# Second and third batch's extensions run back to back in two PSUM banks, and the third's sums are moved into the second's unit

## What is computed

```python
y = einsum('bti,oi->bto', x, W) + b + 2 * einsum('btr,bro->bto', einsum('bti,bir->btr', x, A[slot]), B[slot])
logits = einsum('bsd,ed->bse', y, route_w)
topk_v, topk_idx = top_k(logits, 1)
route_weight = one_hot(topk_idx[..., 0], 8) * topk_v
h = einsum('bsd,erd->bser', y, A2)
out = x + einsum('bser,eor->bso', route_weight[..., None] * h, Bw)
```

## Time and profile before

| | |
|---|---|
| Median of three executions | 285.2 us |
| The profiled execution | 284.73 us |
| Its span in the trace | 282.9 us |
| Mean granted TensorE clock | 0.998 of full speed |
| TensorE matmul, weight load | 277.5 us, 220.6 us busy |
| VectorE, ScalarE, GpSimd | 200.5, 110.2, 15.0 us busy |
| HBM read, written | 54.60 MB, 33.55 MB |

### The profile page before, as it was taken

How to read it: one execution, slowest core, us unless ns; L and a number is a source line. 1 busy time by engine, 2 the same in 40 slices (tenths; PEclk the granted TensorE clock), 3 DMA queues, 4 the chain that set the end, 5 groups by cost and what they waited for, 6 DMA issues and landing times.

```text
span 282.9 us, 4102 instructions
## 1 busy us (share of the span) xinstructions
PE 277.5 (98%) x1602; PEld 220.6 (78%) x1602; DVE 200.5 (71%) x223; ACT 110.2 (39%) x151; POOL 15.0 (5%) x46
## 2 busy tenths in 40 slices
PE   8999999999999999999999999999999999999993
PEld 5999999997676885788588758867885888588882
DVE  0052100077498999699879969996998799788794
ACT  0001201197685542744275346426533743370000
POOL 7600030000000000000000000000000000000000
PEclk9999999999999999999999999999999999999999
DMA  7999999999991076949966993999399759606598
GB/s 241 400 408 396 398 411 412 378 397 414 422 423 82 14 285 204 389 142 385 400 263 226 426 389 152 351 402 398 139 368 396 322 173 423 284 14 259 226 379 323
DMA packets 19014, 88.50 MB, mean 313 GB/s; under 512 B 2346, under 2 KB 4530, under 8 KB 11442
## 3 DMA queue, kind: packets, MB, share of 16 engines
q1 hardware_dynamic: 15696, 83.70, 75.3%
q10 hardware_dynamic: 3298, 4.54, 4.4%
HBM read 54.60 MB, written 33.55 MB: 312 GB/s over the span
## 4 chain that ended last, share of the span: by engine, by line
PE 93%; DVE 5%; ACT 0%; issue 0%; DVEq 0%
PE bank_out L641 16%; PE bank_eh L753 11%; PE bank_eh L769 10%; PE bank_eh L786 10%; PE bank_eh L741 10%; PE bank_out L721 9%; PE bank_out L714 9%; PE bank_out L705 9%; DVE x_ring L625 4%; PE bank_rl L641 3%; PE bank_eh L641 3%; PE bank_rl L679 1%; PE bank_eh L668 1%; PE bank_eh L792 1%; PE bank_rl L791 1%; PE bank_rl L797 1%
## 5 line engine op out<-in xcount | busy, mean ns | idle before, releaser
L393 ACT ACTIVATE x_hi<-x_ring 128x1024 fp32r<-128x1024 f32 x64 | 67.3, 1061 | 54.2 <-PE bank_eh L786 53.8
L489 DVE TENSOR_TENSOR x_lo<-x_ring,x_hi 128x1024 fp32r<-128x1024 f32 x64 | 77.6, 1221 | 8.5 <-ACT x_hi L393 8.5
L578 DVE TENSOR_TENSOR x_ring<-bank_out,x_ring 128x1024 f32<-128x1024 f32 x54 | 65.8, 1218 | 2.9 <-PE bank_out L721 2.7
L753 PE MATMUL bank_eh<-x_hi,m_hi 128*128 128x512 f32 x128 | 50.7, 396 | 0.0
L769 PE MATMUL bank_eh<-x_lo,m_hi 128*128 128x512 f32 x128 | 49.9, 390 | 0.0
L786 PE MATMUL bank_eh<-x_hi,m_lo 128*128 128x512 f32 x128 | 49.8, 389 | 0.0
L705 PE MATMUL bank_out<-wh_hi,bw_hi 128*128 128x512 f32 x120 | 46.7, 389 | 0.0
L714 PE MATMUL bank_out<-wh_lo,bw_hi 128*128 128x512 f32 x120 | 46.7, 389 | 0.0
L721 PE MATMUL bank_out<-wh_hi,bw_lo 128*128 128x512 f32 x120 | 46.7, 389 | 0.0
L641 PE MATMUL bank_out<-pt,w_ring 128*128 128x136 f32 x288 | 34.6, 279 | 0.0
L641 PEld LDWEIGHTS bank_out<-pt,w_ring 128*128 128x128 f32 x288 | 33.9, 190 | 0.1
(11 more groups left out here) (91 smaller groups left out, 211.4 us busy)
## 6 DMA issues: line engine op xcount, KB each, us to landing
x_ring<-xT SPq DMA_DIRECT2D x32, 1024.0 KB, 7.1
outT<-x_ring SPq DMA_DIRECT2D x26, 1024.0 KB, 4.9
w_ring<-W SPq DMA_DIRECT2D x28, 512.0 KB, 11.0
outT<-x_ring SPq DMA_DIRECT2D x5, 512.0 KB, 2.8
outT<-x_ring ACTq DMA_DIRECT2D x4, 512.0 KB, 2.9
w_ring<-W SPq DMA_DIRECT2D x6, 256.0 KB, 5.7
outT<-x_ring SPq DMA_DIRECT2D x5, 256.0 KB, 2.6
x_ring<-loraB ACTq DMA_DIRECT2D x8, 128.0 KB, 10.4
```

The costliest lines, as they stand in the source:

```text
L393: act.activation(out, in_, ACT.Copy).then_inc(done, 1)
L489: dve.tensor_tensor(out, a, b, ALU.subtract).then_inc(done, 1)
L578: dve.tensor_tensor(x, out_bank(b, j)[:, :, :], x, ALU.add).then_inc(v_out, 1)
L753: mm(bank_h, m_hi[:, c, :], hi, start=(c == 0), stop=False)
```

## The change

The batches are counted from 0, so the second and third are b = 1 and b = 2 (`TWIN`). The extension of b = 2 is moved from its own unit to directly behind that of b = 1. For that the extensions use two banks by turns: even batches the old `bank_e`, odd ones what was `bank_r`. The counts go to `bank_l`, over the logits. Top, sum_two, odd, sum_all, the copies to `e_st` and split_e of b = 2 leave the unit of b = 2 and are done in the unit of b = 1, top and sum_two at j = 3 (`TWIN_AT`), odd and sum_all at j = 4, the copies and split_e at j = 5. On ScalarE each of these stands ahead of the part's other work, on VectorE behind it. On VectorE the split of pair 3 of batch 2 is put behind weigh of batch 1. Waits on TensorE follow: the one for weigh of batch 1, which stood in the extension of b = 2, is now ahead of the last matmul of output pair 7 of batch 0; those of the counts' bank are merged with those of the logits.

```diff
@@ -162,8 +162,7 @@
...
         bank_rl = psum("bank_rl", [P, 2, T])
-        bank_e, bank_h = bank_eh[:, 0, :], bank_eh[:, 1, :]
-        bank_r, bank_l = bank_rl[:, 0, :], bank_rl[:, 1, :]
+        bank_e, bank_h, bank_l = (bank_eh[:, 0, :], bank_rl[:, 0, :]), bank_eh[:, 1, :], bank_rl[:, 1, :]
         bank_out = [psum(f"bank_out{i}", [P, 2, T]) for i in range(2)]
@@ -226,6 +225,7 @@
...
         EHI_AT, ELO_AT = 1, 1
+        TWIN, TWIN_AT = 2, 3
         LOG_AT, COPY_AT, AHEAD_AT, COUNT_AT, W_AT = 3, 4, 5, 6, 7
@@ -422,8 +422,8 @@
...
                     act.wait_ge(t_pb, 1)
-                    copy(pb[:, E:XN], bank_r[0:1, 0:PN], a_bp)
-                    copy(pb[:, 0:E], bank_r[0:1, 0:E], a_bp)
+                    copy(pb[:, E:XN], bank_e[1][0:1, 0:PN], a_bp)
+                    copy(pb[:, 0:E], bank_e[1][0:1, 0:E], a_bp)
                     act.wait_ge(a_bp, 4)
@@ -448,24 +448,40 @@
...
-            for b in range(NB):
+            def top(b):
                 act.wait_ge(t_ext, b + 1)
...
                     act.wait_ge(v_two, b)
-                act.activation(e_top[:, :], bank_e[2 * GROUP:4 * GROUP, :], ACT.Identity,
+                act.activation(e_top[:, :], bank_e[b % 2][2 * GROUP:4 * GROUP, :], ACT.Identity,
                                bias=e_bias[:, 0:1]).then_inc(a_top, 1)
+
+            def odd(b):
+                act.wait_ge(v_two, b + 1)
+                if b >= 1:
+                    act.wait_ge(v_sum, b)
+                copy(e_odd[:, :], e_two[GROUP:2 * GROUP, :], a_odd)
+
+            def stack(b):
+                act.wait_ge(v_sum, b + 1)
+                if b >= 1:
+                    act.wait_ge(t_stack, b)
+                copy(e_st[0:GROUP, :], e_sum[:, :], a_ehi)
+                copy(e_st[2 * GROUP:3 * GROUP, :], e_sum[:, :], a_ehi)
+
+            for b in range(NB):
+                if b != TWIN:
+                    top(b)
                 for j in range(NP2):
-                    if j == 0:
-                        act.wait_ge(v_two, b + 1)
-                        if b >= 1:
-                            act.wait_ge(v_sum, b)
-                        copy(e_odd[:, :], e_two[GROUP:2 * GROUP, :], a_odd)
-                    if j == EHI_AT:
-                        act.wait_ge(v_sum, b + 1)
-                        if b >= 1:
-                            act.wait_ge(t_stack, b)
-                        copy(e_st[0:GROUP, :], e_sum[:, :], a_ehi)
-                        copy(e_st[2 * GROUP:3 * GROUP, :], e_sum[:, :], a_ehi)
+                    if j == 0 and b != TWIN:
+                        odd(b)
+                    if j == EHI_AT and b != TWIN:
+                        stack(b)
+                    if j == TWIN_AT and b + 1 == TWIN:
+                        top(TWIN)
+                    if j == TWIN_AT + 1 and b + 1 == TWIN:
+                        odd(TWIN)
+                    if j == TWIN_AT + 2 and b + 1 == TWIN:
+                        stack(TWIN)
                     if j == COPY_AT:
@@ -533,7 +549,7 @@
...
                     dve.wait_ge(a_odd, b)
-                dve.tensor_tensor(e_two[:, :], bank_e[0:2 * GROUP, :], e_top[:, :], ALU.add).then_inc(v_two, 1)
+                dve.tensor_tensor(e_two[:, :], bank_e[b % 2][0:2 * GROUP, :], e_top[:, :], ALU.add).then_inc(v_two, 1)
@@ -557,7 +573,7 @@
...
                 dve.wait_ge(t_count, b + 1)
-                dve.scalar_tensor_tensor(out=wh[:, :], in0=bank_r[:, :], scalar=0.0, in1=wh[:, :],
+                dve.scalar_tensor_tensor(out=wh[:, :], in0=bank_l[:, :], scalar=0.0, in1=wh[:, :],
                                          op0=ALU.is_ge, op1=ALU.mult).then_inc(v_w, 1)
@@ -591,10 +607,10 @@
...
                 for j in range(NP2):
-                    if j == 0:
+                    if j == 0 and b != TWIN:
                         sum_two(b)
                         sum_all(b)
-                    if j == ELO_AT:
+                    if j == ELO_AT and b != TWIN:
                         split_e(b)
@@ -604,12 +620,20 @@
...
                         split_lo(b, SRING + j)
-                    elif b + 1 < NB:
+                    elif b + 1 < NB and (b + 1, j) != (TWIN, NP2 - 1):
                         split_lo(b + 1, j - SRING)
...
                         add_x(b - 1, j - 1)
+                    if j == TWIN_AT and b + 1 == TWIN:
+                        sum_two(TWIN)
+                    if j == TWIN_AT + 1 and b + 1 == TWIN:
+                        sum_all(TWIN)
+                    if j == TWIN_AT + 2 and b + 1 == TWIN:
+                        split_e(TWIN)
                 if b >= 1:
                     weigh(b)
+                if b + 1 == TWIN:
+                    split_lo(TWIN, NP2 - 1 - SRING)
                 if 1 <= b < NB - 1:
@@ -681,7 +705,7 @@
...
             pe.wait_ge(v_pb, C)
-            mm(bank_r[:, 0:PN], ones[:, :], pb_sum[(C - 1) % 2][:, :], start=True, stop=True).then_inc(t_pb, 1)
+            mm(bank_e[1][:, 0:PN], ones[:, :], pb_sum[(C - 1) % 2][:, :], start=True, stop=True).then_inc(t_pb, 1)
             for n in range(BP_AT, NWP):
@@ -697,14 +721,14 @@
...
-                ext_next = b + 2 if j == NP2 - 1 and b + 2 < NB else None
+                ext_next = b + 2 if j == NP2 - 1 and TWIN < b + 2 < NB else None
                 hi, lo = wh_hi[b % 2][:, :], wh_lo[b % 2][:, :]
...
                     if ext_next and i == 0:
-                        pe.wait_ge(a_top, ext_next)
+                        pe.wait_ge(a_top, ext_next - 1)
                     if ext_next and i == 1:
@@ -713,20 +737,20 @@
...
                     if ext_next and i == 0:
-                        pe.wait_ge(v_two, ext_next)
+                        pe.wait_ge(v_two, ext_next - 1)
                     if (b, j, i) == (NB - 2, NP2 - 1, 0):
...
                         pe.wait_ge(v_wh, NB)
+                    if (b, j, i) == (TWIN - 2, NP2 - 1, 1):
+                        pe.wait_ge(v_wh, TWIN)
                     last = mm(out, bw_lo[:, o], hi, start=False, stop=True)
...
-            pe.wait_ge(g_ext, 1)
-            for b in range(NB):
-
+            def extension(b):
                 for r in range(C // NGROUPS):
@@ -736,11 +760,19 @@
...
                             pe.wait_ge(v_m, NWB)
-                        if c == C - 1 and b >= 2:
+                        if c == C - 1 and b > TWIN:
                             pe.wait_ge(v_wh, b)
-                        last = mm(bank_e[g * GROUP:(g + 1) * GROUP, :], ext[b % 2][:, c, :], x_pair(b, c // 2)[:, c % 2, :],
+                        last = mm(bank_e[b % 2][g * GROUP:(g + 1) * GROUP, :], ext[b % 2][:, c, :], x_pair(b, c // 2)[:, c % 2, :],
                                   start=(r == 0), stop=(r == C // NGROUPS - 1))
                 last.then_inc(t_ext, 1)
+
+            pe.wait_ge(g_ext, 1)
+            for b in range(NB):
+
+                if b != TWIN:
+                    extension(b)
+                if b + 1 == TWIN:
+                    extension(TWIN)
@@ -754,23 +786,19 @@
...
                             if b >= 1:
-                                pe.wait_ge(a_log, b)
+                                pe.wait_ge(v_w, b)
                             else:
...
                         if j == COUNT_AT and i == 0:
-                            if b >= 1:
-                                pe.wait_ge(v_w, b)
-                            else:
+                            if b == 0:
                                 pe.wait_ge(a_beats, 3)
...
                         if j == LOG_AT and i == 0:
-                            if b >= 1:
-                                pe.wait_ge(v_ahead, b)
-                            else:
+                            if b == 0:
                                 pe.wait_ge(v_glo, 3)
@@ -778,7 +806,7 @@
...
                             else:
-                                pe.wait_ge(g_ext, 2)
+                                pe.wait_ge(g_ext, TWIN + 1)
                         if b == 1 and j == 1 and i == 1:
@@ -794,7 +822,7 @@
...
                         pe.wait_ge(v_ahead, b + 1)
-                        mm(bank_r, beats[:, :], ahead[:, :], start=True, stop=True).then_inc(t_count, 1)
+                        mm(bank_l, beats[:, :], ahead[:, :], start=True, stop=True).then_inc(t_count, 1)
                 if b >= 1:
...
                         out_pair(b - 1, j)
```

## The result

The changed kernel takes 291.54 us (median of six runs, 290.55 to 292.18) against 285.19 us for the kernel before: ratio 1.0223, 95% interval 1.0203 to 1.0243. It is slower, as forecast, but by 6.35 us and not by 4.6, and lies 0.6 us above the upper end of the range.

A forecast was written before the change was run, and what follows sets the result against it. TensorE's own gapless matmul work was taken as the bound. Stalls of 5.13 us less 0.33 gained gave 4.8 slower; 4.6 was taken, so 285.2 + 4.6 = 289.8 us, range 287.2 to 290.9 (main forecast alone 288.8 to 290.5).

The forecast's parts named there:

- The gain, 0.33 us: Joining two extensions in one run saves one entry and exit on TensorE: 3.76 + 3.43 instead of 2 x 3.76 us.
- Edits at no cost: Third extension's weights, batch 2's input, bank and wait changes, and reloads were claimed hidden, adding nothing to the time.
- The exchange: Batch 2's sums in batch 1's unit make VectorE and ScalarE wait in turn; late additions stall TensorE 5.13 us.
- the walk: Tracing the engines' in-order queues through batch 1's unit with old durations: stalls 0.66, 2.61, 1.72, 0.14 us; net 4.8 slower.
- the lower middle between two ways of spacing VectorE's instructions: VectorE spacing of 1.13 us throughout would give 4.1 us slower, full 1.22 us each 5.2; 4.6 was taken.
- the clock falls too: Rival: TensorE's clock also drops at the stalls and stays down 3.60 us, 1.8 us more: 291.6 us, 5%.
- The rival's 1.8 us: Extra cost if TensorE's clock fell for as long as eight warm-up matmuls (3.60 us, 0.45 each instead of 0.23); 5%.
- The rival of a cover that holds: Slack at output pairs 5 and 6 absorbs VectorE's delay, leaving only the 0.33 us gain: 284.9 us, 8%.

## Why the prediction was right or wrong

- **The gain, 0.33 us.** Right. Alone it measures 0.36 to 0.37 us in the loop. The run of 64 narrow matmuls takes 7.01 us to the first wide one (83.59 to 90.60) where one extension took 3.57 (110.05 to 113.62): the second adds 3.44 us, against the 3.43 of its eight sets.
- **Edits at no cost.** Right. TensorE did not wait for the load of batch 2's x, whose tail ends near 88 in this profile too, nor for the extension's weights. The first reload went out at 117.1 us, 8.7 later than in the earlier trace rows; no x_hi waited for it. Banks and waits alone measured nothing.
- **The exchange.** Right in place, and 0.4 us too small in size: breaks of 2.48 and 1.78 us against 2.5 and 1.8, stalls ahead of pairs 5, 6 and 7, each starting pair within 0.3 us of its place in the walk. The stalls and their restarts come to 4.97 us net (changed kernel with three matmuls' fill) against 4.8 in the walk and 4.6 taken. Taking the lower middle between two ways of spacing VectorE's instructions was the worse choice here; the walk itself gave 4.8, and the restarts, 0.11 us each (0.34 instead of 0.23), were left out. For the addition that follows the compare, with only x_lo between them, the walk had 1.24 us from the start of x_lo, and the profile agrees: x_lo and that addition start at 111.13 and 112.38, 1.25 us apart, where the pair with no compare ahead of it is 1.14 apart (105.68, 106.82).
- **The clock.** Wrong, and the step that failed. The sum has no term for it: I gave "the clock falls too" 5% and left its 291.6 us out of the range; measured were 291.54. What was wrong was the reading of the earlier trace rows: that row shows a clock at 0.50 some 4 us after the last matmul (which starts at 278.08), and I took the shorter stalls of my walk to be safe by it. It shows nothing of shorter ones. The clock fell behind 2.31 us of idleness in the changed kernel and behind 1.79 us in the one without the moved sums, with dense matmuls ahead of both. The changed kernel's profile shows two levels: 0.43 us from matmul to matmul at a granted clock of 0.50 (114.60 to 121.40), 0.23 us at 0.99 to 1.00 around it.
- **The price of a fall.** The rival's 1.8 us came out (1.5 by the ratios, 1.8 by the medians, 1.9 by the loop), but by luck. It supposed 3.60 us at the lower level, after the warm-up matmuls of the earlier trace rows. The lower level lasted 6.8 us, nearly twice that, and pair 7's wait hid a part of it. Nor do those rows show that the clock was low at the start; the matmuls are 0.45 us apart there, but the granted clock of that stretch reads 1.00 in the kernel before:

```profile
1.00:4.60 3.60, 3.60 (x9) 1.58 (x10) 0.00 (x0) 0.00 (x0) 3.08 (x11) 1.00 0.71 233
```

- **The rival of a cover that holds** was wrong for the order that was chosen, and holds with another: 284.6 us.

What stays open: why the clock fell in these runs and not in the others. It fell behind idle stretches of 2.31 us (five runs of six) and 1.79 us (four of five); it did not behind 1.61 and 1.54 us in one kernel, or 1.43 us with two short ones ahead, in any of four runs each. The lengths are those of the one profiled run of each kernel. As the same kernel ran with and without a fall, the length of the stall is not shown to be all that decides.

## What to carry to other kernels

Where two in-order engines hand a small piece of work back and forth, each handover must stand behind the work that the other engine needs next, or both wait for each other in turn (here ScalarE 3.09 and 3.08 us, VectorE 2.48 and 1.78); look not at how busy an engine is but at what stands behind its wait. A walk through the queues with durations of the old trace finds such stalls to 0.3 us, and is worth making before the edit. When the engine that stalls is TensorE and a walk gives idle stretches like the 1.79 and 2.31 us here, give the fall of the clock a real chance and a price of its own. Where the wait can't be removed, a few matmuls that nobody reads may be cheaper than the idle time: all three fills that were run here made their kernel faster, by 1.4, 1.8 and 1.2 us between the medians.

## What the runs showed of the hardware that was not expected

An idle stretch of 1.79 us in an otherwise dense stream of matmuls was followed within about 1.1 us of work by 3.4 us at a granted clock of 0.51 (matmuls 0.43 us apart), and in another kernel 2.31 us were followed by 6.8 us at 0.50. With three matmuls (0.68 us) put into the longer of them the clock stayed at 1.00 (110 to 122 us of the profiled run) and the kernel was 1.5 to 1.9 us faster.
